# Banded attention with queries and keys kept in two orders, one two-bank unit of near and far blocks per head

## The reference

```
OFFSETS = sorted(set(range(0, 33)) | {48, 64, 96, 128, 192, 256, 384})
scores = stack([einsum('bhnd,bhnd->bhn', q, shift(k, delta)) for delta in OFFSETS]) * scale + pos_bias
alpha  = softmax(where(n < delta, -inf, scores))
out    = sum_i alpha[..., i] * shift(v, OFFSETS[i])
gate   = sigmoid(x @ Wgate + bgate);  result = (flat(out) * gate) @ Wout + bout
```

## Time and profile before

| | us |
|---|---|
| median of 3 runs | 3774.55 (3772.28 to 3777.3) |
| the profiled execution: its time | 3782.0 |
| the profiled execution: its span | 3780.3 |
| banded attention, first transpose to last output | 83.46 to about 1619 |
| PE busy | 3176.4 (84% of the span) |
| DVE / ACT / POOL busy | 1747.6 (46%) / 1189.4 (31%) / 352.9 (9%) |

### The profile page before, as it was taken

The page is one execution under the profiler, slowest core; times in us unless marked ns, Lnnn a source line. Parts: engine busy times, 40 slices in busy tenths (PEclk is TensorE's granted clock), DMA queues, the critical chain, the costliest instruction groups (busy, mean ns, idle before and its releaser), DMA issues. The chain is left out here.

```text
span 3780.3 us, 99336 instructions
## 1 busy us (share of the span) xinstructions
PE 3176.4 (84%) x44860; PEld 1864.3 (49%) x44860; DVE 1747.6 (46%) x3244; ACT 1189.4 (31%) x1486; POOL 352.9 (9%) x334
## 2 busy tenths in 40 slices
PE   1688888888788888879957899999999898997898
PEld 0456565656565666634443444444444444443345
DVE  5334333434333333361074665666666656664302
ACT  0122222222222222232002545554545554553300
POOL 0000000000000000000002111121212121100000
PEclk9788888888788888789957999999999999998896
DMA  5422222222222222126813222222222222312394
GB/s 131 109 68 74 68 74 68 74 71 71 71 71 68 74 68 74 33 92 266 359 15 84 52 52 60 56 56 52 52 53 59 52 60 52 68 19 93 124 419 175
DMA packets 235041, 343.30 MB, mean 91 GB/s; under 512 B 115962, under 2 KB 144452, under 8 KB 218244
## 3 DMA queue, kind: packets, MB, share of 16 engines
q1 hardware_dynamic: 222452, 334.40, 30.9%
q10 hardware_dynamic: 12176, 2.66, 0.5%
HBM read 266.15 MB, written 69.24 MB: 89 GB/s over the span
## 5 line engine op out<-in xcount | busy, mean ns | idle before, releaser
L1351 DVE TENSOR_REDUCE b_tops<-b_slot 128x8 f32<-128x1024 f32 x576 | 680.4, 1220 | 361.5 <-PE b_slot L1208 182.6
L1388 ACT ACTIVATE b_probs<-b_slot 128x1024 f32<-128x1024 f32 x576 | 583.1, 1023 | 551.2 <-PE b_slot L1208 395.5
L711 DVE TENSOR_TENSOR a_probs<-a_scores,a_bias_k 128x512 f32<-128x512 f32 x256 | 176.6, 690 | 554.5 <-PE a_scores L570 318.3
L803 ACT ACTIVATE a_probs<-a_probs 128x512 f32<-128x512 f32 x256 | 161.5, 631 | 589.7 <-DVE a_probs L711 588.6
L1228 PE MATMUL b_outT_ps<-b_probs,b_v 128*17 128x128 f32 (+3 forms) x4608 | 318.0, 384 | 6.2 <-ACT b_probs L1388 5.5
L1208 PE MATMUL b_slot<-b_q_stack,b_k_stack 99*128 99x512 bf16 (+3 forms) x1280 | 275.8, 322 | 43.3 <-DVE b_tops L1351 32.8
L1208 PE MATMUL b_slot<-b_k_stack,b_q_stack 96*128 96x512 bf16 (+3 forms) x1280 | 267.1, 323 | 29.4 <-DVE b_tops L1351 20.6
L1155 POOL TENSOR_SCALAR_AFFINE_SELECT b_probs<-b_probs 128x1024 f32<-128x1024 f32 x128 | 139.8, 1093 | 809.5 <-ACT b_probs L1388 809.5
L1208 PEld LDWEIGHTS b_slot<-b_q_stack,b_k_stack 99*128 99x128 bf16 x1280 | 107.2, 100 | 204.6 <-DVE b_tops L1351 61.9
L1208 PEld LDWEIGHTS b_slot<-b_k_stack,b_q_stack 96*128 96x128 bf16 x1280 | 97.6, 98 | 185.4 <-DVE b_tops L1351 61.6
L1762 PE MATMUL f_ps<-f_w_ring,f_hidT 128*32 128x256 f32 x1024 | 184.0, 381 | 2.1 <-ACT f_hidT L1803 2.1
(11 more groups left out here) (215 smaller groups left out, 4492.1 us busy)
## 6 DMA issues: line engine op xcount, KB each, us to landing
f_w_ring<-in_L_ffn_w_dram SPq DMA_DIRECT2D x128, 1024.0 KB, 10.1
parts_dram<-a_parts SPq DMA_DIRECT2D x96, 256.0 KB
parts_dram<-b_parts SPq DMA_DIRECT2D x96, 256.0 KB
a_k_stack<-parts_dram SPq DMA_DIRECT2D x128, 128.0 KB, 3.0
b_k_stack<-parts_dram SPq DMA_DIRECT2D x64, 256.0 KB, 7.1
a_q_stack<-parts_dram SPq DMA_DIRECT2D x64, 192.0 KB, 3.0
b_q_stack<-parts_dram SPq DMA_DIRECT2D x32, 384.0 KB, 4.6
values_dram<-a_v_stage SPq DMA_DIRECT2D x32, 272.0 KB, 2.6
```

The source lines that it names most:

```text
L711: dve.tensor_tensor(dst[:, :].rearrange("p (t c) -> p t c", c=64), src[:, :].rearrange("p (t c) -> p t c", c=64), bias_k[k][:, HG * g + h, ...
L803: act.activation(dst[:, :], dst[:, :], ACT.Exp).then_inc(probs_ready, 1)
L1351: ins = dve.tensor_reduce(out, src, AX.X, ALU.max)
L1388: act.activation(probs_of(b, g, u, h)[:, :], slot_of(step)[:, :], ACT.Exp).then_inc(taken_act, 1)
```

## The change

Queries and keys are kept twice, once by token and once by residue, so that near and far products both read neighbouring columns. POOL makes the second order (`turn`: three copies of 128x1024 for each half of q or k), and spill and stack DMAs carry both. Near and far blocks of a head become one unit of 128x1024 in two banks; PSUM is three such slots for all uses and `outT_ps`. The projection gives 1024 columns at a time; the two subtractions go from DVE to POOL (`rest1`, `part2`), and the first part is rounded from `full`, which shares its memory with `zb` and `flatT`. `parts` exists once, for q and k alike; the stacks hold two heads each, in a ring of three. The maxima get rows in both orders (`mt`: 16 products of 12x128, read by ACT and DVE; `mrow`: four DMAs). `v_near`, `v_far`, `v_stage` and the probabilities exist once. The list of steps is written anew.

```diff
     def projections(b, half):
         out = []
         for which in "qk":
-            for step in (which, "part1", "part2"):
-                out += [(step, b, half, c) if step == which else (step, b, half, c, which) for c in range(2)]
-            out.append(("spill", b, half, which))
+            out += [(which, b, half)] + [(step, b, half, which) for step in ("part0", "rest1", "part1", "part2", "turn", "spill")]
         return out
...
+            if g == 1:
+                first += [("z", b + 1, 0), ("zt", b + 1, 0), ("z", b + 1, 1), ("zt", b + 1, 1)]
+            if g in (1, 3):
+                p = projections(b + 1, g // 2)
+                last = p + last if g == 1 else last
+                first = first + p[0:7] if g == 3 else first
+                last = p[7:] if g == 3 else last
+            if g == 2:
+                v = values(b + 1)
+                first += v[0:2]
+                last += v[2:4]
+        return first, last
+
+    seq = [("z", 0, 0), ("zt", 0, 0), ("z", 0, 1), ("zt", 0, 1)] + projections(0, 0)
+    seq += operands(0) + operands(1) + operands(2) + projections(0, 1) + values(0)
+    seq += [("mx", 0, 0, h) for h in range(HG)] + [("fparts", 0, 0), ("fp", 0, 0), ("mred", 0, 0), ("mt", 0, 0), ("mrow", 0, 0)]
...
+            seq += [("vin", b, g), ("S", b, g, 0)] + tops[0] + [("S", b, g, 1)] + operands(n + 3) + tops[1]
+            seq += first[cuts[0]:cuts[1]] + [("S", b, g, 2)] + first[cuts[1]:cuts[2]] + [("S", b, g, 3)] + operands(n + 4)
+            seq += first[cuts[2]:cuts[3]] + tops[2] + tops[3] + ([("fparts",) + after] if more else [])
+            seq += near + ([("fp",) + after, ("mred",) + after] if more else [])
+            seq += far[0:4] + ([("mt",) + after, ("mrow",) + after] if more else []) + far[4:8]
+            seq += last + [("ote", b, g)]
...
+                    elif kind == "rest1":
+                        _, b, half, which = step
+                        pool.wait_ge(part0_done, count("part0", "part0", b, half, which))
+                        pool.tensor_tensor(full, full, parts[:, 0, 0, :], ALU.subtract).then_inc(rest1_done, 1)
...
+                    elif kind == "turn":
+                        _, b, half, which = step
+
+                        pool.wait_ge(part2_done, count("part2", "part2", b, half, which))
+                        for part in range(PARTS):
+                            pool.tensor_copy(parts[:, part, 1, :].rearrange("p (r a) -> p r a", r=LINKS),
+                                             parts[:, part, 0, :].rearrange("p (a r) -> p r a", r=LINKS)).then_inc(turned, 1)
...
-                        sp.wait_ge(part2_done, count("part2", "part2", b, half, 1, which))
+                        sp.wait_ge(turned, PARTS * count("turn", "turn", b, half, which))
...
-                            sp.dma_start(scratch["parts"].ap()[m, half, :, part], parts[m][:, part, :]).then_inc(spilled[m], 16)
+                            sp.dma_start(scratch["orders"].ap()[m, half, :, part], parts[:, part, :, :]).then_inc(spilled, 16)
...
+                        sp.wait_ge(v_out, 16 * count("vout", "vout", b, 1))
+                        if prev := before(b, g):
+                            sp.wait_ge(pv_done, count("PV", "PV", *prev, 1, NT - 1))
...
-                            ins = pe.matmul(dst[RES * r2:RES * (r2 + 1), 64 * pair:64 * (pair + 1)],
-                                            left[rows, h, r:N:LINKS], right[rows, h, r:N:LINKS],
-                                            start=start, stop=True, skip_group_check=True)
+                    for r in range(LINKS):
+                        pair, r2 = divmod(r, 2)
+                        at = 512 + 64 * pair
+                        ins = pe.matmul(dst[RES * r2:RES * (r2 + 1), at:at + 64], left[rows, h, 1, RES * r:RES * (r + 1)],
+                                        right[rows, h, 1, RES * r:RES * (r + 1)], start=start, stop=True, skip_group_check=True)
...
+                    elif kind == "part0":
+                        _, b, half, which = step
+                        act.wait_ge(taken_dve, count("taken_dve", which, b, half))
+
+                        hold(act, spilled, SPILL * (count("part0", *step) - 1))
+                        act.activation(parts[:, 0, 0, :], full, ACT.Copy).then_inc(part0_done, 1)
```

More of the change, by code:

```diff
@@ L172, in maxima @@
-    def maxima(b, g):
-        far = [("mx", b, g, 1, h) for h in range(HG)]
-        near = [("mx", b, g, 0, h) for h in range(HG)]
-        return [far[0:2], near[0:2], far[2:4] + [("fparts", b, g)], near[2:3], near[3:4] + [("fp", b, g)],
-                [("mred", b, g)], [("mt", b, g), ("mrow", b, g)], []]
-    def outputs(b):
-        return [[("ot", b, 3, 0), ("ot", b, 3, 1)], [("gmul", b), ("at", b, 0), ("at", b, 1)],
-                [("op", b, 0), ("at", b, 2), ("op", b, 1)], [("at", b, 3), ("op", b, 2), ("op", b, 3)]]
@@ L223, in others @@
-        if g == 3 and b < B - 1:
-            v = values(b + 1)
-            for u in range(4):
-                out[u] += v[2 * u:2 * u + 2]
-            out[5].append(("vin", b + 1, 0))
-        return out
-    seq = tokens(0) + projections(0, 0)
-    for g in range(2):
-        seq += operands(0, g, 0) + operands(0, g, 1)
-    seq += values(0) + [("vin", 0, 0)]
-    for steps in maxima(0, 0):
-        seq += steps
-    left = []
+            first = [("ot", b - 1, 3), ("gmul", b - 1), ("at", b - 1, 0), ("op", b - 1, 0), ("at", b - 1, 1), ("op", b - 1, 1)] if b else []
@@ new lines, in others @@
+            return first, [("gate", b, 0), ("gate", b, 1)]
+        first, last = [("ot", b, g - 1)], []
+        if g == 1 and b:
+            last += [("stats", b - 1, i4) for i4 in range(2)]
+        if b < B - 1:
+            if g == 1:
[9 more added lines that the diff above has]
+                last += v[2:4]
@@ L466, in band_attention, with slot_of @@
+        stacked = [sem(f"stacked{n}") for n in range(3)]
+        SPILL, STACK, VIN = 16 * PARTS, 16 * sum(len(runs(which)) for which in range(2)), 16 * 6
+        MROW = 16 * HG
+        N_CLEARED = 2 + 1 + 3 + 3 + 1
+        def slot_of(step):
+            return slots[(nth["filled", step] - 1) % 3]
         with nc.Block() as block:
@@ L562, in products @@
[L562 to L578 removed]
+                        by = users[n]
```

614 lines of the change are left out of this document (282 added, 332 removed).

## The result

| | before | after |
|---|---|---|
| median (us) | 3775.85 of 4 runs (3772.28 to 3777.3) | 4297.86 of 4 runs (4286.99 to 4307.42) |
| ratio, 95% interval | | 1.1383 [1.1355, 1.1412] |
| first scores of the stage | 140.5 | 233.5 |
| `gmul` of sequences 0, 6, 7 | 347.2, 1477.8, 1599.9 | 468.7, 1960.5, 2118.6 |
| a whole sequence (mean of six), the period | 188.4 | 248.6 |

The kernel is 522 us slower; 3938 was forecast, with a range up to 4060. The direction was right, the time was outside the range. The first scores come 93.0 later, sequence 0 takes 28.6 more from there to its `gmul`, six sequences 361.2, the last interval 35.9: 519 in all.

What follows compares the result with a forecast made beforehand. PE was taken to set the pace. Start-up +74, sequence 0 +4, six sequences +92 and the last part -6 gave +164 on 3782.0, 3946, or 3938 as median; own range 3860 to 4020, with rivals 3740 to 4060.

Steps and rivals of the forecast that it cites:

- stays: 7.9: Banded loop: what remains of PE's idle time was taken to stay, 7.9 us a sequence.
- What bounds it, and PE's gain: Banded loop: PE sets the pace; contiguous far units take 0.35, saving 0.82 each, -26 us a sequence.
- Far units unchanged, the last rival: Far units stay at 1.17 for their 64x64 shape, PE gains nothing: about 4146 us, chance 0.04.
- PE's clock: Loop: longer waits lower the granted clock, +2 us a sequence.
- The main term: Group 1: chain of q and k through turns, spills and single `parts` delays `ote` and stack, +33 a sequence (23 to 40).
- The other stacks: Group 3: one late stack charged at 2 us a sequence, within 16 for that group's new waits.
- the contention rival: Stacks, values and doubled spills meet on the DMA engines, +20 for seven sequences: 4078 us, chance 0.10.
- Instructions for PE: Near and far `PV`: no new wait for instructions was sized; the remaining idle time, 7.9 a sequence, was kept.
- Rows of maxima: Wait from `mt`, 6.1, hidden in groups 0 to 2 behind gate, q and k, v: 8.8 a sequence go.
- Start-up: Before the first scores: the chain runs four times unhidden, first scores at 214 against 140.5, +74 (50 to 90).
- Sequence 0: First sequence of the loop: +15.4 less 11 for the half moved to the start-up, +4 us.
- the last interval -6: Last 122.2 us, without projections: -21 + 2 for PE, +10 two late stacks, +3 `at` and `op`: -6.

Runs made afterwards that it cites:

- e6: Kernel before, far products reading 64 neighbouring columns for both operands in place of every 16th (wrong tokens): 3631.95 us, 0.9616.
- e14: e13 with spills and stacks carrying only the order by token, half the bytes (wrong tokens): 3834.93 us, 1.0162 to the kernel before.
- e11: e9 with q's spill placed behind the rows of maxima in the list: 3942.79 us, 1.0429 to the kernel before.
- e1: Changed kernel with `ote` ahead of the projections' chain in the list: 4282.97 us, 1.1332 to the kernel before.
- e2: Changed kernel with k's spill held back behind the next group's first stack load: 4111.7 us, 1.0871 to the kernel before.
- e3: Changed kernel with both edits, `ote` first and k's spill late: 4062.05 us, 1.075 to the kernel before.
- e4: Changed kernel with spills and stacks carrying only the order by token, half the bytes (wrong tokens): 4011.97 us, 1.0632 to the kernel before.
- e13: e11 with each group's first stack load asked for ahead of q's spill and the values: 3988.49 us, 1.0552 to the kernel before.
- e5: e3 with the large products (gate, q, k, v) placed between the pieces of `PV`: 4009.56 us, 1.0608 to the kernel before.
- e9: e3 with a reordered list start, `fp`, `mred` and `mt` earlier in near `PV`, a large product after each: 3999.36 us, 1.058 to the kernel before.

## Why the forecast came out 360 us low

Two steps of the prediction failed. It left PE's supply of instructions at nothing: near and far `PV` were taken as the same work in another order, inside the idle time that "stays: 7.9". Measured were 28.3 a sequence in all lines, 26.6 of them in `PV`, against 6.7 before. And it took the transfers of 1.5 MB as shorter than they are (a spill 8.5, measured 12.2) and the other stacks, but for 2 us, as hidden (8.6 and 3.9 in two more groups): stacks and `ote` cost 53.3 where 44 was forecast.

Per whole sequence (six of them):

| | forecast | measured |
|---|---|---|
| PE busy | 138.5 (159.5 - 26 + 3 + 2) | 146.9 |
| stacks and `ote` | about 44 (33 + 3 + 3 + 3 + 2) | 53.3 |
| PE without instructions in `PV` | in the 7.9 that stays | 26.6 |
| other waits | 21.3, these 7.9 among them | 21.8 |
| sum | 203.8 | 248.6 |

- **What bounds it, and PE's gain: right.** The far unit was forecast at 0.35 and has a pitch of 0.37 at full clock (911.29 to 911.66); its weight loads take 122 to 131 ns, where near 103 was named as the sign. e6 gives 27.1 of busy time a sequence against 26. Far units unchanged, the last rival, is out.
- **PE's clock: mis-sized.** +2 was forecast for longer waits; the granted clock fell from 0.84 to 0.74 over the six sequences. With the same number of products e14 has 0.82 and 137.3 busy a sequence. So some 10 of the 146.9 are the lower clock (an estimate), and over the runs it is lowest where PE idles most (0.74 at 41% idle, 0.78 at 30% in e11, 0.84 at 15% before). That was to be sized from the forecast's own 65 of waits, not as a small term.
- **The main term: right in mechanism, short in size.** 33 was forecast, 38.8 measured in the sequence shown (16.3 + 22.5). e1, e2 and e3 show that it is one chain and that the stack's place in the queue ends it. Its durations were short. The spill: the trace had 6.4 for 0.75 MB and I took 8.5 for twice as much; it is 12.2, beyond the upper bound of 11.6, and e4's 7.0 shows that it goes nearly by bytes. Each turn: 4.9 was taken, 6.0 measured. Behind k's turn as much again was missed: the issue of its spill took 4.0 for 2.0, that of the values 7.6 for 3.7, and the stack landed 13.4 behind its issue for 10.1. So the stack came 15 later than forecast, and the wait grew by 6 only because PE stood in other waits meanwhile (3.9 and 2.6 for DVE) and ran slower: part of how near 38.8 is to 33 is luck.
- **The other stacks: a step that failed.** I charged one late stack (2) and took the rest as hidden. Beside the 22.5 there are 8.6 and 3.9 in groups 3 and 0. This is the contention rival in a milder form and with another cause: e2 and e13 show the queue's order, e4 and e14 the bytes. Both are true. With the bytes doubled each repair of the order moves the wait to the next transfer (`ote`, stack, rows, stack, exponentials); what would free the loop in full was not found.
- **Instructions for PE: the step that failed by most.** I read near and far `PV` as the same work in another order; 21.6 of the 44.8 that a sequence came out too low are here (28.3 - 6.7). Before, S and `mx` units and far `PV` alternated, and PE was without instructions for 17.3 us of six sequences in those lines; now 520 products of 10 to 25 ns follow one another. Spread among large products the gaps lose a third (e5), with half the bytes a third (e4); e14, with both, has 5.8 a sequence left in `PV` and 5.2 in the near and far units, 13.0 in all lines; part of its `PV` waits for exponentials instead. That the gaps are the supply itself the landings on queue q8 show; what the rest of them would need isn't shown.
- **Rows of maxima: right.** Their 8.8 went. In e5 and e9 they came back, once the steps around `mt` had moved and q's spill stood ahead of them on SP.
- **Start-up: right in its chain, short in size.** First scores at 233.5 against 214, from four spills of 12.2 for 8.5. Sequence 0 was given +4 and has +28.6, the last interval -6 and has +35.9: both by the same stacks and gaps (for sequence 0, 39.6 for stacks and 25.8 without instructions). I had sized them from the loop's gain and not from its waits. Of the signs, PE's 59% in the loop, the waits at `ot` and at the third `mx` and the first scores past 200 came as named; ACT's wait at `part0` was 20.4 for 12 to 16, the DMA share 0.42 for near 0.50.

The error is mostly the per-sequence term, 45 us too low in each of six sequences, with 42 in the last interval, 25 in sequence 0 and 19 in the start-up.

**A rule of the skill.** The contiguous copy takes 1.04 us and the one with a 32-byte step 2.03 (medians; the means shown, 1162 and 2187 ns, have a few long ones in them). The Trainium skill (GPSIMD Engine Reference, Performance pitfalls for Q7 kernels) says that a read from SBUF with a step over 8 bytes costs about half as much again. The measurement decides: here it is 1.9 times.

## What to carry to other kernels

Twice the bytes took 1.7 times as long to land here (12.2 for 7.0), and a change that makes operands cheap for one engine by sending them twice must be priced by the queue that carries them. Read the list of the DMA-issuing engine as a schedule of its own: a step that waits there (a spill for its turn) delays every transfer behind it, and moving that one step was worth 186 us. When a wait is taken away, name the next in line before counting the gain.

## What the runs showed of the hardware

- **TensorE can run out of instructions.** A transfer of 16.4 KB holds 128 products with their weight loads. The transfers start at least 3.3 us apart and take 1.1 (median), and PE goes on some 1.4 behind the landing, while 128 small products of `PV` run in 1.2 (far) to 1.9 us (near) at full clock. Spreading them among products with more columns took the gaps from 27.7 to 18.6 us a sequence.
- **The weights' step alone is the smaller part.** Products of 64 by 64: 313 ns with both scattered, 296 with contiguous weights, 206 with both contiguous; the moving operand alone wasn't run.
- **A spill lands nearly by its bytes:** 7.0 us for 0.75 MB, 12.2 for 1.5 MB.
- **Issue is slower right behind a spill:** four DMAs of the values took 6.25 us to issue there, 2.48 at 771.44 with none ahead and 2.44 before. Small DMAs behind it land later too: PE went on 9.2 us after the issue of the rows of maxima, 4.4 where they stood ahead of it (e9, e11). The runs don't show why.
- **POOL and DVE slow each other.** In the changed kernel a copy of the turn stands beside `gmul` (DVE, 128x2048 from two operands in SBUF) in each of seven sequences: `gmul` takes 3.0 to 4.1 us there, 2.29 in the eighth without one and in the kernel before, and the copy 4.15 for 2.03.
